# A causal depthwise convolution inside a Mamba stage: diagonal matmuls on TensorE replaced by tap instructions on VectorE

## The reference

```python
xz = jnp.einsum('bld,ed->ble', x, in_proj_w)
u, z = jnp.split(xz, 2, axis=-1)                     # 512 channels each
conv = lax.conv_general_dilated(u_t, conv_w[:, None, :], (1,), [(D_CONV - 1, 0)], ...,
                                feature_group_count=D_INNER)   # 4 taps, one filter per channel
u = jax.nn.silu(conv + conv_b)
dbc = jnp.einsum('bld,ed->ble', u, x_proj_w)         # -> dt (rank 16), B (16), C (16)
dt = jax.nn.softplus(dt @ dt_proj_w + dt_proj_b);  A = -jnp.exp(A_log)
s = s * jnp.exp(dt * A) + (dt * u) * B;  y = sum_n(s * C)      # scan over the sequence, 16 states
y = (y + u * D_skip) * jax.nn.silu(z);  out = y @ out_proj_w.T
```

## Time and profile before

| | us |
|---|---|
| median of three executions | 2692.03 |
| lowest, highest | 2681.50, 2698.86 |
| the profiled execution | 2698.86 |
| its span, first to last instruction | 2697.2 |
| Mamba loop, first scan to last scan | 65.3 to 1101 |
| mean granted TensorE clock | 0.914 |

### The profile page before, as it was taken

The page is one execution under the profiler, slowest core; times in us unless marked ns, Lnnn a source line. Parts: engine busy times, 40 slices in busy tenths (PEclk is TensorE's granted clock), DMA queues, the critical chain, the costliest instruction groups (busy, mean ns, idle before and its releaser), DMA issues. The chain is left out here.

```text
span 2697.2 us, 48685 instructions
## 1 busy us (share of the span) xinstructions
PE 2361.1 (88%) x16893; PEld 1599.6 (59%) x16893; DVE 1931.1 (72%) x4282; ACT 1506.9 (56%) x3353; POOL 1309.6 (49%) x1257
## 2 busy tenths in 40 slices
PE   6769888889898986879999978898896999999797
PEld 2446565656565565557777756565663666566555
DVE  1999999999999999336667647777755545466545
ACT  4677778777878775333333324444444666655522
POOL 0777777787868686333333224444444232221401
PEclk8769899999998998989999988999957999899899
DMA  5444344444444444020000134243203000000100
GB/s 159 150 130 147 126 146 132 145 130 147 130 147 128 146 127 135 30 74 1 1 1 1 24 75 73 50 77 65 51 2 104 16 18 22 17 18 17 49 14 9
DMA packets 138502, 204.64 MB, mean 76 GB/s; under 512 B 24417, under 2 KB 59362, under 8 KB 138130
## 3 DMA queue, kind: packets, MB, share of 16 engines
q1 hardware_dynamic: 136274, 198.64, 25.4%
q0 software_dynamic: 960, 2.62, 0.3%
q10 hardware_dynamic: 1024, 0.26, 0.1%
HBM read 161.29 MB, written 14.68 MB: 65 GB/s over the span
## 5 line engine op out<-in xcount | busy, mean ns | idle before, releaser
L426 POOL TENSOR_TENSOR ma_seen<-ma_state,ma_cs 128x1024 f32<-128x1024 f32 x256 | 603.1, 2360 | 294.6 <-DVE ma_state L1032 288.0
L1032 DVE TENSOR_TENSOR_SCAN ma_state<-ma_decay,ma_last,ma_drive 128x512 f32<-128x512 f32 x512 | 650.5, 1271 | 4.6 <-ACT ma_decay L873 4.6
L1019 DVE TENSOR_TENSOR ma_drive<-ma_weight,ma_bs 128x512 f32<-128x512 f32 x512 | 357.3, 698 | 36.8 <-ACT ma_weight L863 4.4
L639 PE MATMUL ma_acc<-ident,ma_seen 128*128 128x128 f32 x2048 | 294.4, 294 | 68.2 <-POOL ma_seen L426 68.1
L639 PEld LDWEIGHTS ma_acc<-ident,ma_seen 128*128 128x128 f32 x2048 | 259.4, 153 | 157.2 <-POOL ma_seen L426 93.1
L873 ACT ACTIVATE ma_decay<-ma_dt,ma_a_neg 128x512 f32<-128x512 f32 x512 | 338.2, 709 | 0.0
L2138 DVE CUSTOM_DVE_ANT_0 sw_score<-sw_score,both_band 128x256 f32<-128x256 f32 (+1 forms) x512 | 197.6, 448 | 68.7 <-PE sw_score L1952 57.8
L2076 ACT ACTIVATE sw_prob<-sw_turned 128x512 f32<-128x512 f32 (+1 forms) x256 | 135.5, 581 | 191.2 <-PE sw_turned L1966 174.6
L104 POOL TENSOR_TENSOR moe_h_low<-both_V,light_wqkv 128x512 fp32r<-128x512 f32 x80 | 104.8, 1310 | 245.7 <-DVE light_wqkv L100 238.2
L1874 POOL TENSOR_SCALAR_AFFINE_SELECT sw_prob<-sw_prob 128x512 f32<-128x512 f32 x128 | 84.3, 659 | 227.2 <-ACT sw_prob L2076 227.2
L1598 DVE TENSOR_TENSOR both_V<-both_V,moe_up 128x512 f32<-128x512 f32 x80 | 55.0, 688 | 118.7 <-PE moe_up L1387 73.7
(11 more groups left out here) (551 smaller groups left out, 5632.7 us busy)
## 6 DMA issues: line engine op xcount, KB each, us to landing
ma_bs<-bc_rows SPq DMA_DIRECT2D x256, 256.0 KB, 3.2
ma_cs<-bc_rows SPq DMA_DIRECT2D x256, 256.0 KB, 3.2
ma_h<-kept_taps SPq DMA_DIRECT2D x28, 256.0 KB, 4.1
both_wide<-both_kh SPq DMA_DIRECT2D x28, 192.0 KB, 4.1
both_wide<-both_qh SPq DMA_DIRECT2D x20, 256.0 KB, 4.8
x_rows<-X SPq DMA_DIRECT2D x1, 4096.0 KB
light_rows<-li_y SPq DMA_DIRECT2D x32, 128.0 KB, 1.9
out_dram<-li_o SPq DMA_DIRECT2D x32, 128.0 KB, 1.8
```

The costliest lines, as they stand in the source:

```text
L426: g.tensor_tensor(out=seen[n % RR][:, :, :], in0=state[n % SR][:, :, :], in1=each(cs[n % CR][:, :], 2), op=ALU.mult).then_inc(S["seen_full ...
L639: ins = t.matmul(accs(j, mm), seen[n % RR][:, mm, j * P:(j + 1) * P], K["ident"][:, :], is_transpose=True, start=False, stop=(last_ and j ...
L1019: v.tensor_tensor(out=drive[mm][:, :], in0=weight[mm][:, :], in1=bs[n % CR][:, :], op=ALU.mult).then_inc(S["drive_done"], 1)
L1032: v.tensor_tensor_scan(state[n % SR][:, mm, :], decay[s % DR][:, :], drive[mm][:, :], last[:, k, m:m + 1], ALU.mult, ALU.add).then_inc(S[" ...
```

## The change

The convolution leaves PE. In `projected` ACT, after the copy to `ubuf`, makes a second pass over the PSUM bank in place: `bank = w3*bank + b`. DVE then adds the other three taps with `scalar_tensor_tensor`: `bank = w_k*ubuf[k:k+512] + bank` for k = 0 and 1, and the third writes the sum to `pre`. The bank is free for PE's next unit only after the third tap (`emptied` names `conv_done`).

The units `conv` are gone from PE's list; projects move from steps 11 to 14 to steps 11, 12, 14, 15 and ACT's `projected` to steps 12, 13, 15, 16; ACT's `conv_out` is gone. On DVE the taps follow the scans of half-steps 26 to 30 (blocks 0 and 1) and 32 to 36 (blocks 2 and 3), where 28 and 34 have two and the one at 36 stands behind `gate`. With them go the diagonal matrices, their store, their 28 loads and the semaphores. Before the loop, PE runs the four projects in a row and DVE the 12 taps.

```diff
-    if q in (11, 12, 13, 14) and front:
-        found.append(("project", i + 1, q - 11))
-    if q in (13, 15, 16, 17) and front:
-        found.append(("conv", i + 1, (13, 15, 16, 17).index(q)))
+    if q in (11, 12, 14, 15) and front:
+        found.append(("project", i + 1, (11, 12, 14, 15).index(q)))
...
-    order = [("turn1", 0, k) for k in range(DH)] + [("project", 0, 0)]
-    for m in range(1, MB):
-        order += [("project", 0, m), ("conv", 0, m - 1)]
-    order += [("conv", 0, MB - 1), ("rows", 0, 0), ("steps", 0, 0), ("steps", 0, 1)]
+    order = [("turn1", 0, k) for k in range(DH)] + [("project", 0, m) for m in range(MB)] + [("rows", 0, 0), ("steps", 0, 0), ("steps", 0, 1)]
...
-    return {"turn1": ("xT1_full", DH * i + k + 1), "project": ("u_out", MB * i + k + 1), "conv": ("conv_done", MB * i + k + 1), "rows": ("dbc_out", i + 1),
+    return {"turn1": ("xT1_full", DH * i + k + 1), "project": ("conv_done", MB * i + k + 1), "rows": ("dbc_out", i + 1),
...
-            def taps_again(f, m):
-
-                if m == 0:
-                    sp.wait_ge(S["taps_stored"], 16)
-                    sp.wait_ge(S["conv_done"], MB * f)
-                    since(sp, "x1_full", GT * (f - 1))
-                    since(sp, "h2_done", HB * (f - 2))
-                sp.dma_start(h1[:, m, :], kept_taps[:, m, :]).then_inc(taps_in[m], 16)
-
-            sp.wait_ge(S["taps_made"], MB * CONV)
-            sp.dma_start(kept_taps[:, :, :], h1[:, :, :]).then_inc(S["taps_stored"], 16)
...
-                if n // Q < LAST and n % Q in (10, 11, 12, 13):
-                    taps_again(n // Q + 1, n % Q - 10)
...
-            def conv(f, m):
-
-                pe.wait_ge(S["u_out"], MB * f + m + 1)
...
-                for k in range(CONV):
-                    ins = t.matmul(out[:, :], tap_of(m, k), ubuf[:, m, k:k + GN], start=(k == 0), stop=(k == CONV - 1))
-                fill(ins, "conv", f, m)
...
                 a.activation(ubuf[:, m, CONV - 1:], out[:, :], ACT.Copy).then_inc(S["u_out"], 1)
-
-            def conv_out(f, m):
-                out = filled("conv", f, m)
-                since(act, "dt_done", 2 * f)
-                a.activation(pre(m // 2)[:, m % 2, :], out[:, :], ACT.Identity, bias=conv_b[:, m:m + 1]).then_inc(S["conv_done"], 1)
+                a.activation(out[:, :], out[:, :], ACT.Identity, scale=conv_w[:, m, CONV - 1:CONV], bias=conv_b[:, m:m + 1])\
+                 .then_inc(S["conv_in"], 1)
...
-                    if q in (12, 13, 14, 15) and front:
-                        projected(i + 1, q - 12)
-                    if q in (14, 16, 17, 18) and front:
-                        conv_out(i + 1, (14, 16, 17, 18).index(q))
+                    if q in (12, 13, 15, 16) and front:
+                        projected(i + 1, (12, 13, 15, 16).index(q))
...
+            def tap(f, m, k):
+
+                b, turn, before = TURN["project", f, m]
+                n = (CONV - 2) * (MB * f + m)
+                if k == 0:
+                    dve.wait_ge(S["conv_in"], MB * f + m + 1)
+                else:
+                    dve.wait_ge(S["conv_step"], n + k)
+                taps = lambda out: v.scalar_tensor_tensor(out=out, in0=ubuf[:, m, k:k + GN], scalar=conv_w[:, m, k:k + 1],
+                                                          in1=bank[b][:, :], op0=ALU.mult, op1=ALU.add)
+                if k < CONV - 2:
+                    taps(bank[b][:, :]).then_inc(S["conv_step"], 1)
+                else:
+                    since(dve, "dt_done", 2 * f)
+                    taps(pre(m // 2)[:, m % 2, :]).then_inc(S["conv_done"], 1)
...
+                        if front:
+                            for m, first in enumerate((26, 28, 32, 34)):
+                                if 0 <= 2 * q + mm - first < CONV - 1:
+                                    tap(i + 1, m, 2 * q + mm - first)
...
             for m in range(MB):
-                for k in range(CONV):
-                    v.tensor_scalar(tap_of(m, k), K["ident"][:, :], conv_w[:, m, k:k + 1], None, ALU.mult).then_inc(S["taps_made"], 1)
+                v.tensor_scalar(diag_skip[:, m, :], K["ident"][:, :], skip[:, m:m + 1], None, ALU.mult).then_inc(S["diags"], 1)
             for m in range(MB):
-                v.tensor_scalar(diag_skip[:, m, :], K["ident"][:, :], skip[:, m:m + 1], None, ALU.mult).then_inc(S["diags"], 1)
+                for k in range(CONV - 1):
+                    tap(0, m, k)
```

More of the change, by code:

```diff
@@ L295, in mamba_phase @@
         pre = lambda h: (ramp, ex)[h]
-        tap_of = lambda m, k: h1[:, m, k * P:(k + 1) * P]
-        kept_taps = nc.dram_tensor("kept_taps", (P, MB, CONV * P), F32).ap()
         bc_rows = nc.dram_tensor("bc_rows", (GROUPS, 2 * NS, GN), F32).ap()
@@ L306, in mamba_phase @@
             "x_first", "x_rest", "w_first", "w_in", "a_exp", "ln_raw", "ln_one", "a_neg", "made", "diags", "stat3", "root_in1", "root_in2", "root_in3",
-            "squared1", "rstd1_done", "xs1_full", "xT1_full", "halo", "u_out", "taps_made", "taps_stored", "conv_done", "u_full", "b_step", "b_split",
+            "squared1", "rstd1_done", "xs1_full", "xT1_full", "halo", "u_out", "conv_in", "conv_step", "conv_done", "u_full", "b_step", "b_split",
             "dbc_out", "rows_stored",
@@ L313, in mamba_phase @@
         b_in, c_in = ([A.sem(f"{n}{k}") for k in range(CR)] for n in ("b_in", "c_in"))
-        taps_in = [A.sem(f"taps{m}_in") for m in range(MB)]
         bank_full = [A.sem(f"bank{k}_full") for k in range(2)]
@@ L400, in _ @@
             sp.wait_ge(S["x_rest"], 16)
-            for m in range(MB):
-                sp.wait_ge(taps_in[m], 16 * LAST)
             for k in range(CR):
@@ L548, in project @@
                 fill(ins, "project", f, m)
-            def conv(f, m):
-                pe.wait_ge(S["u_out"], MB * f + m + 1)
-                if f == 0:
-                    pe.wait_ge(S["taps_made"], CONV * (m + 1))
-                else:
-                    pe.wait_ge(taps_in[m], 16 * f)
-                out = take("conv", f, m)
-                for k in range(CONV):
-                    ins = t.matmul(out[:, :], tap_of(m, k), ubuf[:, m, k:k + GN], start=(k == 0), stop=(k == CONV - 1))
-                fill(ins, "conv", f, m)
             def rows(f):
@@ L666, in body @@
                             project(j, k)
-                        if kind == "conv":
-                            conv(j, k)
                         if kind == "turn2":
@@ L679, in _ @@
             turn1(0, 1)
-            project(0, 0)
-            for m in range(1, MB):
+            for m in range(MB):
                 project(0, m)
-                conv(0, m - 1)
-            conv(0, MB - 1)
             pe.wait_ge(S["diags"], MB)
@@ L962, in _ @@
             halos(0)
-            projected(0, 0)
-            for m in range(1, MB):
+            for m in range(MB):
                 projected(0, m)
-                conv_out(0, m - 1)
-            conv_out(0, MB - 1)
             convolved(0)
```

## The result

| | before | after |
|---|---|---|
| median, us (seven executions of each on one chip) | 2681.8 | 2703.1 |
| lowest, highest | 2679.1, 2700.5 | 2698.5, 2720.9 |
| ratio, with its 95% interval | | 1.0055 [1.0036, 1.0076] |
| the profiled execution | 2698.9 | 2709.1 |
| first scan starts | 65.3 | 55.6 |

The change makes the kernel slower by 0.55%, which on 2681.8 us is 14.8 us, with bounds of 9.7 and 20.4. The two medians lie further apart, 21.3 us or 0.79%, which is above that interval. The ratio lies near that of the means (1.0056 for all 34 executions of after against the seven of before), and three of the seven of before took 2692 us or more. Within the Mamba stage the change costs 17.4 us in these two profiles, where 23.6 were predicted: the loop is 27.1 us longer and starts 9.7 us earlier. The same two kernels profiled again, further down, give 20.2 us.

What follows compares the result with a forecast made beforehand. DVE was taken to bound the Mamba loop (983.8 of 1036 us busy). Taps +46.8, new waits +1.6, removed waits -17.3 and earlier start -7.5 gave +23.6 us on 2692.0: forecast 2716 us, range 2700 to 2742.

Steps and rivals of the forecast that it cites:

- case A: Whole kernel: DVE pays for the taps, ACT waits go, the start comes earlier; +23.6 us, 2716 us; chance 0.67.
- on the median the sum gives 2715.6: Whole kernel: +23.6 us added to 2692.0, the median of three executions of before, as the forecast.
- together 17.3 us: DVE in the loop: waits for ACT that go, 11.7 us for gz, 4.6 for decays, 1.0 for weight.
- gap rule: DVE's loop: a tap alone in its gap adds 0.52 us, a second or one behind the gate 0.67; 46.8 us altogether.
- New waits: DVE's first tap of block 0 waits for ACT's bias pass: 1.2 us in group 6, 0.2 in groups 1 and 3; 1.6 total.
- In front of the loop: Before the first scan: DVE taps replace PE's convolution, saving 8.6 us at fast clock, 6.3 at slow; 7.5 taken.
- Chance of slower by over 1%: Whole kernel: chance 0.44 of over 1% slower, from a third of A (0.23) and nearly all of B and C (0.21).
- B: PE in the loop turns late behind held banks, its clock drops, the 17.3 us of waits stay; +40.9, 2733 us; chance 0.12.
- A granted clock well under 0.90: PE in the loop: a granted clock this low was listed as a sign that the prediction was wrong.
- C: DVE's loop: each tap waits for the one before, no overlap; taps 58.6 us, total +35.4, 2727 us; chance 0.11.
- D: DVE's loop: taps stream two elements a cycle at 0.435 us; total -2.9, 2689 us; chance 0.05.
- E: Loop: PE sets the pace and taps fill DVE's 52.2 us of holes; total -1.8, 2690 us; chance 0.05.

Runs made afterwards that it cites:

- relief only: The changed kernel without the 84 taps in the loop, against before: ratio 0.9921 [0.989, 0.9952], first to last scan 1014.5 us.
- bunched kernel: The changed kernel with a block's three taps in one gap instead of three, against before: ratio 1.0104 [1.0064, 1.0145], first to last scan 1073.5 us.
- one-source cost kernel: Before plus 84 unused taps on DVE in the loop, one source in PSUM, PE's convolution kept: ratio 1.009 to before, first to last scan 1056.2 us.
- two cost kernels: Before plus 84 unused DVE taps in the loop: both sources in SBUF, ratio 1.0168; one source in PSUM, ratio 1.009.

## Why the prediction was right in its mechanism and wrong in its size

The mechanism was the one predicted, case A: the taps are paid in full by DVE, the waits for ACT go, the start comes earlier, and the sum stays within 1%. The time of 2703.1 us lies in the range of 2700 to 2742 but 12.5 under the forecast of 2716.

What failed is the size of terms. The step that failed most is the base of the sum, "on the median the sum gives 2715.6". It took 2692.0, the median of three executions that lay 17 us apart, for what before takes. The seven beside after have 2681.8, so this step alone is 10.2 us of the 12.5; against that base the forecast of 2716 means +34, and +14.8 to +21.3 were measured. The step that failed next is "together 17.3 us" for the waits that go: it kept 2.6 us of the waits for weight without a reason given, and all 19.9 went.

The +23.6 itself lies outside the interval of the first measurement (+14.8 [9.7, 20.4]) and inside that of the second (1.0064 is +17 [9, 26]). At the last scan the two pairs of profiles show +17.4 and +20.2. All terms are of the right sign, three of four err to the slow side, and for the first pair they add up:

| term | predicted | measured | by |
|---|---|---|---|
| 84 taps in the loop | +46.8 | +44.5 | rows of after, scan to drive |
| taps wait for ACT | +1.6 | +2.0 | DVE's waits |
| waits that go | -17.3 | -19.4 | loop's +27.1 less the two above; relief only gave -19.5 to -20.0 |
| in front of the loop | -7.5 | -9.7 (-7.3 in the repeats) | first scan |
| sum | +23.6 | +17.4 (+20.2 in the repeats) | last scan |

- **Tap.** Taken 0.75, it was 0.72 to 0.74 on the median, and neighbours overlap by 0.09 us where 0.08 was taken. The lower of the two estimates, from the half-sized row and the slope, had said 0.73. Over 84 taps two hundredths matter: 2.3 us.
- **Overlap.** The gap rule worked from the earlier trace rows held: 0.49 for the predicted 0.52, 0.65 for 0.67. The pipe rule of the Trainium skill (VectorE: DVE Perf Modes, The DRAIN you can't avoid) agrees with the bunched kernel, where dependent taps stand in a row without overlap. Its strict form does not agree with after, where the tap that follows the gate starts 1.12 us into the gate's 1.20, and by itself it does not price the tap in a gap.
- **Waits.** All of gz and decay went, as predicted for groups 0 to 6. The failing step is the waits for weight: 1.0 us was to go, and all three of before (3.6) went, while two new ones brought 0.8. A second, smaller one is what a removed wait returns: I took the recorded idle time, but the instruction then also overlaps the one in front by some 0.09 us (the gate starts 1.19 behind the start of a scan of 1.27). Against it stand 1.4 us more of waits behind DVE's own scans. An estimate from these rows: 19.9 less 0.8 less 1.4, and 16 overlaps of 0.09, is 19.1, and the 19.4 are what is left over in the loop.
- **New waits.** 2.0 us for 1.6, but in other groups than said. Group 4, where I worked out nothing, waited 1.00 us [the row at 643.91]; group 6, where I worked out 1.2, had none, and groups 1 to 3 had 0.70, 0.18 and 0.15. ACT's bias pass was 0.75 us where I took 0.69, and the offsets between ACT and DVE were read from before, and the change moves them. The size of the term was luck.
- **In front of the loop.** I worked out 8.6 us for the fast clock and 6.3 for the slow one and took 7.5. Both projects came at the fast clock (1.96 us for four passes, against 1.88 at 25.29 in the earlier trace rows) and the table load at 31.25, as the fast case said (31.3); the eight matmuls of the rows behind, 5.28 us in after and 6.26 in that execution of before, gave one more. Before profiled again has 5.30 there and its first scan at 63.0, and the saving is then 7.3, within 0.2 of the 7.5. So the miss of 2.2 in the table is in good part the spread of before's first scan (63.0 to 65.3 us in the five profiles with its convolution in front of the loop), and the 7.5 was a choice of the middle that no run confirms or refutes.
- **Chance of slower by over 1%.** One result cannot say that 0.44 was too much, but it came from a sum that stood 3 us under the 1% mark, and its steps that were off went the same way: 0.75 for 0.73, recorded idle for returned time, and waits kept that went.

The rivals. **B** was half right: the granted clock of the loop fell to 0.85, and PE stood 49 us for the taps. "A granted clock well under 0.90" was named as a sign of being wrong; it came, and it was a poor sign. For the waits for gz did not stay, so its decisive point was not reached, and the slower PE cost nothing: it had 237 us (1058 less 820.9) without work in the loop. **C** was refuted as the change stands and priced by the bunched kernel. **D** fell with taps of 0.73. **E** fell with the one-source cost kernel (+21.7 us with PE's work kept) and with relief only, where DVE's loop got 20 us shorter without any convolution on PE: that is what its lateness was worth of the 52 us. Most of the rest lies in the 461 half-steps of before in which the drive starts 1.34 us behind the start of a scan of 1.27, 32 us in all.

## What to carry to other kernels

Where one engine sets the pace, price moved work by what it adds between the neighbours at that very place, since a single instruction in a gap costs less than its duration (0.49 us of 0.73 here) and dependent ones in a row nearly the whole of it (2.07 of 2.28 for three). Work that hurts in a steady loop can pay in front of it, where the other engine is the one on the path: try the two places apart before judging the whole change. Take the base of a forecast from more executions than three when they lie further apart than the change is worth. A wait that an engine shows names the first instruction that asked, so moving that one shifts the wait and does not remove it.

## What the runs showed of the hardware that was not expected

In this kernel an instruction of DVE with both tensors in SBUF was held up while POOL worked on SBUF tensors: 718 ns at best and 2104 at worst for the same 128x512 instruction, mean 934 over 84; with one of the two in PSUM, 715 to 746. The Trainium skill (SBUF — State Buffer, Who interferes with whom) has a DVE instruction with two SBUF inputs contend with a GpSimd instruction that reads SBUF, and calls the shared port pair an exclusive lock. The trace agrees for the tap at 660.09: POOL's product had 1.27 us left, and 1.27 + 0.72 - 0.09 is 1.90 where 1.82 was recorded. It agrees the other way round as well. The tap at 663.62 came first and took 0.72, and the product that POOL began during it took 2.69 in place of 2.36:

```profile
663.87 2.69 POOL L426 TENSOR_TENSOR ma_seen<-ma_state,ma_cs 128x1024 f32<-128x1024 f32 x1 [2.51 <-DVE ma_state L1034]
```

POOL's 256 products took 612.3 us in that kernel and 603.1 in before. By an estimate from the two cost kernels, taps with both sources in SBUF would have cost some 17 us more (84 x 0.21).

The stages behind the loop, whose code is the same in all these kernels, took 1577 to 1603 us. Part of it shows in the sliding-window stage, with PE's clock. First before, then after, 102 us of each (columns as above):

```profile
1900.00:2002.00 102.00, 95.79 (x993) 68.11 (x993) 70.71 (x326) 45.52 (x95) 46.06 (x89) 0.73 0.17 33
```

```profile
1900.00:2002.00 102.00, 89.96 (x1186) 63.17 (x1180) 83.73 (x386) 56.22 (x120) 57.23 (x112) 0.98 0.24 44
```

PE had a granted clock of 0.73 in the one and 0.98 in the other. It got through 993 and 1186 instructions, in part because the stage starts 16 us later in after, so that the window shows another piece of it. The stage as a whole, by DVE's instructions on the scores, took 408.6 us in before and 399.2 in after:

```profile
L2138 DVE CUSTOM_DVE_ANT_0 sw_score<-sw_score,both_band x512: 289/465/468, 1593.1 to 2001.7; 128x256 f32<-128x256 f32 x160, 128x128 f32<-128x128 f32 x11
```

```profile
L2110 DVE CUSTOM_DVE_ANT_0 sw_score<-sw_score,both_band x512: 289/465/469, 1609.4 to 2008.6; 128x256 f32<-128x256 f32 x160, 128x128 f32<-128x128 f32 x11
```

The repeats of the same kernels showed clocks of 0.75 and 0.98 in that window, and 408.1 and 392.3 us for the stage. It may hang on how the stage is entered, which no run tested; but after and its repeat, both at 0.98, still differ by 12 us behind the loop, 7 of them in this stage. What decides it stays open. For a change of half a per cent, the last scan is the better yardstick than the end of one profiled execution.
